# Taylor-softmax attention and a quantised FFN: rows and sums moved through HBM buffers, z formed on ScalarE

## What is computed

```python
h  = layernorm(x) ; h = layernorm(h) * ln_w + ln_b
q, k, v = heads(h @ w_q), heads(h @ w_kv[:, :256]), heads(h @ w_kv[:, 256:])   # 16 heads of 16
q, k = rope(q, theta), rope(k, theta)
s = q @ k.T / 4
t = 1 + s + 0.5 * s * s                    # Taylor instead of exp
x = x + layernorm(((t / t.sum(-1)) @ v) @ w_o)
g = layernorm(x)                           # FFN: both sides to a 6-bit grid in blocks of 32
x = x + layernorm(quant(g) @ quant(weight).T + bias)
```

## Time and profile before

| | |
|---|---|
| time, median of 3 runs | 648.65 us (647.7 to 649.6) |
| the profiled execution's own time | 651.11 us |
| its span, first to last instruction | 648.8 us |
| mean granted TensorE clock | 0.985 of full |
| TensorE, VectorE, ScalarE, GpSimd busy | 615.9, 594.8, 530.0, 449.3 us |
| instructions | 20724 |
| moved by DMA | 43.51 MB in 52362 packets |

### The profile page before, as it was taken

The page is one execution under the profiler, slowest core; times in us unless marked ns, Lnnn a source line. Parts: engine busy times, 40 slices in busy tenths (PEclk is TensorE's granted clock), DMA queues, the critical chain, the costliest instruction groups (busy, mean ns, idle before and its releaser), DMA issues. The chain is left out here.

```text
span 648.8 us, 20724 instructions
## 1 busy us (share of the span) xinstructions
PE 615.9 (95%) x6620; PEld 457.7 (71%) x6620; DVE 594.8 (92%) x1489; ACT 530.0 (82%) x1448; POOL 449.3 (69%) x785
## 2 busy tenths in 40 slices
PE   6889999999999999999999999999999999999974
PEld 5666667676776776777777777767777766788763
DVE  5799899899899989999999999989999999987796
ACT  4347788888788897989888888978888888999973
POOL 3475466677777878788777867767877777765464
PEclk9699999999999999999999999999999999999996
DMA  7101031222223232232323232223223212230201
GB/s 245 34 2 42 20 76 30 72 63 65 50 72 88 70 91 68 75 84 67 62 67 83 77 86 73 69 57 101 60 68 92 76 39 41 68 91 18 68 26 49
DMA packets 52362, 43.51 MB, mean 67 GB/s; under 512 B 7201, under 2 KB 48545, under 8 KB 52257
## 3 DMA queue, kind: packets, MB, share of 16 engines
q1 hardware_dynamic: 51440, 41.42, 24.1%
q10 hardware_dynamic: 816, 0.79, 0.4%
HBM read 18.65 MB, written 8.39 MB: 42 GB/s over the span
## 5 line engine op out<-in xcount | busy, mean ns | idle before, releaser
L1168 ACT ACTIVATE feat<-ps_f 128x512 f32<-128x512 f32 x256 | 144.4, 599 | 4.9 <-PE ps_f L852 4.3
L691 DVE TENSOR_TENSOR kf<-kf 128x896 f32<-128x896 f32 (+1 forms) x128 | 131.2, 1027 | 1.8
L852 PE MATMUL ps_f<-qT,selr 128*128 128x512 f32 x320 | 122.1, 435 | 1.8 <-ACT qT L1236 1.3
L691 POOL TENSOR_TENSOR kf<-kf 128x224 f32<-128x224 f32 x64 | 76.5, 1195 | 13.3 <-DVE kf L1515 11.1
L1015 PEld LDWEIGHTS ps_mt<-kf,vp 128*32 128x32 f32 x2048 | 64.1, 110 | 30.0 <-issue 28.3
L1015 PE MATMUL ps_mt<-kf,vp 128*32 128x153 f32 x2048 | 79.7, 296 | 0.6 <-DVE kf L691 0.6
L1725 POOL TENSOR_TENSOR qsp<-kf,qsp 128x256 fp32r<-128x256 f32 x64 | 58.6, 916 | 9.8 <-ACT qsp L1259 9.6
L852 PEld LDWEIGHTS ps_f<-qT,selr 128*128 128x128 f32 x320 | 52.8, 190 | 15.2 <-issue 11.0
L913 PE MATMUL ps_o<-feat,main 120*32 120x512 f32 x448 | 59.7, 604 | 0.0
L916 PE MATMUL ps_o<-feat,rm 128*32 128x512 f32 x448 | 58.6, 593 | 0.0
L788 PE MATMUL ps_qk<-wkqv_h,hT_l 128*128 128x512 f32 x128 | 52.4, 409 | 3.3 <-DVE wkqv_l L1425 3.3
(11 more groups left out here) (199 smaller groups left out, 1885.2 us busy)
## 6 DMA issues: line engine op xcount, KB each, us to landing
xc<-L_attn_x SPq DMA_DIRECT2D x16, 512.0 KB, 4.5
result<-fin SPq DMA_DIRECT2D x64, 128.0 KB, 2.0
xa<-L_attn_x SPq DMA_DIRECT2D x15, 512.0 KB, 4.1
heads_out<-osb SPq DMA_DIRECT2D x224, 32.0 KB, 2.0
shares<-sums SPq DMA_DIRECT2D x112, 64.0 KB
sums<-osb SPq DMA_DIRECT2D x224, 2.0 KB
wkqv<-L_attn_w_kv ACTq DMA_DIRECT2D x2, 256.0 KB, 4.9
xa<-L_attn_x SPq DMA_DIRECT2D x1, 384.0 KB, 6.2
```

Source lines behind the costliest of these rows:

```text
L691: return eng.tensor_tensor(dims(row, F_MAIN, [[FW, heads], [HD, NR - 1], [1, HD]]), dims(row, F_LIN, [[FW, heads], [0, NR - 1], [1, HD]]), ...
L852: pe.matmul(ps_f[i % 2][:, :], selr[:, i], queries, start=True, stop=True).then_inc(sel_done, 1)
L1168: act.activation(feat[:, p2, i], ps_f[i % 2][:, :], ACT.Square).then_inc(squared, 1)
```

## The change

It has five parts. (1) move_quad stores a whole quad of osb, 256 KB, in one transfer to an HBM buffer rows. After four quads the new fetch_heads reads the sums (one transfer) and the heads (two) from it; the new store_inverses stores the inverted sums to an HBM buffer inverses, and spread_shares reads them from there, each head's row 16 times, in two transfers. That makes 4 + 3 + 1 + 2 = 10 transfers a sequence. copy_quad now waits for the quad's store alone. (2) normalise_x runs on ScalarE as an Identity with a column of scales and one of biases; the bias is minus mean times inverse root, a new GpSimd stage shift_x. (3) constant and rest_terms are cut in two stages each. (4) IDLE has 14 fills of two products in the first steps and one drain near the end. (5) ORDER is new for all engines; the pitch of TensorE's cycle is 58 as before.

```diff
-        "attend": ((43, 54, 65, 76, 90, 101, 114, 127, 140, 154, 168, 183, 198,), (25, 39, 53, 69,), (474, 489, 503,
...
+        "attend": ((43, 55, 67, 78, 87, 104, 114, 126, 139,), (24, 38, 52, 68,), (285, 300, 314, 330, 344, 358, 373,
...
-IDLE = {"fill": (), "drain": ()}
+IDLE = {"fill": (2, 2, 2, 4, 4, 6, 7, 10, 10, 14, 14, 19, 24, 32,), "drain": (943,)}
...
+        rows = nc.dram_tensor("rows", [2, NQ, P, T], F32).ap()
+        inverses = nc.dram_tensor("inverses", [H * T // P, P], F32).ap()
...
+        centre_x = sb("centre_x", [P, 2])
...
+                spread(n, "store_inverses", store_inverses)
+                spread(n, "fetch_heads", fetch_heads)
...
-                par, quad, s = t.par, t.tile, t.seq
-                if quad == 0:
-                    wait(sp, norm_ready, NT * (s - 1))
-                    for tile in range(NT):
-                        wait(sp, shares_in[tile], 16 * CH * s)
+                par, quad = t.par, t.tile
+                wait(sp, heads_in[par], 16 * CH * (t.load - 1))
+                wait(sp, sums_in, 16 * (t.seq - 1))
                 sp.wait_ge(o_copied, t.n)
-                for part in range(NT):
-                    sp.dma_start(sums[part * H + HQ * quad:part * H + HQ * (quad + 1)],
-                                 osb[HD:P:VW, par, quad, part * P:(part + 1) * P]).then_inc(sums_in, 16)
-                for h in range(HQ):
-                    row = HD * (HQ * (quad % 2) + h)
-                    sp.dma_start(heads_out[row:row + HD, par, quad // 2], osb[VW * h:VW * h + HD, par, quad]).then_inc(heads_in[par], 16)
+                sp.dma_start(rows[par, quad], osb[:, par, quad]).then_inc(moved[par], 16)
+            def fetch_heads(t):
+                par, s = t.par, t.seq
+                wait(sp, inverses_out, 16 * s)
+                sp.wait_ge(moved[par], 16 * NQ * t.load)
+                by_row = rows[par].rearrange("q (h r) n -> (q h) r n", r=VW)
+                sp.dma_start(sums[:, :], by_row[:, HD]).then_inc(sums_in, 16)
+                wait(sp, norm_ready, NT * (s - 1))
+                for c in range(CH):
+                    sp.dma_start(heads_out[:, par, c], by_row[c * HC:(c + 1) * HC, 0:HD]).then_inc(heads_in[par], 16)
+            def store_inverses(t):
+                s = t.seq
+                for c in range(CH):
+                    wait(sp, shares_in[c], 16 * s)
+                sp.wait_ge(inverted, s + 1)
+                sp.dma_start(inverses, sums[:, :]).then_inc(inverses_out, 16)
...
                 s = t.seq
+                sp.wait_ge(inverses_out, 16 * (s + 1))
                 wait(sp, norm_ready, NT * s)
-                sp.wait_ge(inverted, s + 1)
-                for tile in range(NT):
-                    for c in range(CH):
-                        first = tile * H + c * HC
-                        sp.dma_start(shares[:, c, tile * P:(tile + 1) * P],
-                                     dims(sums[first:first + HC, 0:1], 0, [[0, HD], [1, P]])).then_inc(shares_in[tile], 16)
+                for c in range(CH):
+                    sp.dma_start(shares[:, c], dims(inverses, c * HC * T, [[0, HD], [1, T]], [T, HC])).then_inc(shares_in[c], 16)
...
+            def normalise_x(t):
+                act.wait_ge(x_centred, t.n)
+                wait(act, zT_done, t.n - 2)
+                act.activation(z[:, t.two, 0:D - 1], xa[:, t.par, t.tile, 0:D - 1], ACT.Identity,
+                               bias=centre_x[:, t.two:t.two + 1], scale=rs["x"][:, t.two:t.two + 1]).then_inc(z_ready, 1)
...
-                wait(act, sums_in, 16 * NQ * NT * (t.seq - 1))
-                wait(act, heads_in[par], 16 * H * (t.load - 1))
+                wait(act, moved[par], 16 * NQ * (t.load - 1))
...
+                each(n, "normalise_x", normalise_x)
...
                 wait(dve, z_ready, t.n - 2)
+                wait(dve, x_centred, t.n - 2)
                 dve.bn_aggr(mv[:, t.two], st[:, t.two]).then_inc(means, 1)
...
-            def normalise_x(t):
-                dve.wait_ge(rstd["x"], t.n)
-                wait(dve, zT_done, t.n - 2)
-                dve.tensor_scalar(z[:, t.two, 0:D - 1], xa[:, t.par, t.tile, 0:D - 1], mv[:, t.two, 0:1], rs["x"][:, t.two:t.two + 1],
-                                  ALU.subtract, ALU.mult).then_inc(z_ready, 1)
...
+            def sum_linear(t):
+                dve.wait_ge(mt_copied, t.seq + 1)
+                wait(dve, cb_ready, t.seq)
+                dve.tensor_reduce(lins[:], mts[:, :, F_LIN:NF], AX.X, ALU.add).then_inc(lins_done, 1)
             def constant(t):
-                dve.wait_ge(mt_copied, t.seq + 1)
-                dve.tensor_reduce(lins[:], mts[:, :, F_LIN:NF], AX.X, ALU.add).then_inc(lins_done, 1)
                 dve.wait_ge(lins_done, t.seq + 1)
...
-            def rest_terms(t):
+            def scale_terms(t):
...
                 dve.tensor_scalar(rest[:, :, HD:VW], mts[:, :, F_LIN:NF], ALPHA / 2, None, ALU.mult).then_inc(lins_scaled, 1)
+            def rest_terms(t):
                 dve.wait_ge(lins_scaled, t.seq + 1)
...
             def invert_sums(t):
-                dve.wait_ge(sums_in, 16 * NQ * NT * (t.seq + 1))
+                dve.wait_ge(sums_in, 16 * (t.seq + 1))
                 dve.reciprocal(sums[:], sums[:]).then_inc(inverted, 1)
...
-                    dve.wait_ge(heads_in[t.par], 16 * H * t.load)
-                    dve.wait_ge(shares_in[t.tile], 16 * CH * (t.seq + 1))
+                    dve.wait_ge(heads_in[t.par], 16 * CH * t.load)
+                    for c in range(CH):
+                        dve.wait_ge(shares_in[c], 16 * (t.seq + 1))
...
             def rstd_x(t):
+                wait(pool, z_ready, t.n - 2)
                 inverse_root("x", t)
+            def shift_x(t):
+                pool.wait_ge(rstd["x"], t.n)
+                wait(pool, z_ready, t.n - 2)
+                pool.tensor_scalar(centre_x[:, t.two:t.two + 1], mv[:, t.two, 0:1], rs["x"][:, t.two:t.two + 1], -1.0,
+                                   ALU.mult, ALU.mult).then_inc(x_centred, 1)
```

More of the change, by code:

```diff
@@ new lines @@
+    "sequence", "scale_ln": "once", "scale_terms": "sequence", "sines": "once", "split_ffn_weight": "once", "split_wo":
+    "once", "spread_shares": "spread", "store_inverses": "spread", "sum_bias": "once", "sum_linear": "sequence",
+    "sum_wo": "once", "tables": "once", "turn_attention": "tail", "turn_ffn_weight": "once", "turn_quads": "tail",
+    "turn_sums": "sequence", "turn_weights": "once", "warm_up": "once", "weight_cast_high": "once", "weight_cast_low":
+    "once", "weight_choice": "once", "weight_distance_sizes": "once", "weight_distances": "once", "weight_high": "once",
```

504 lines of the change are left out of this document (257 added, 247 removed), and 96 rows, old and new, of the table ORDER.

## The result

The changed kernel took **658.1 us** (median of 4 runs, 655.0 to 659.5) where the kernel before took 648.2 beside it: a ratio of 1.015, 95% interval 1.0098 to 1.0202. It is slower by 1.5%; the forecast was 633 us, its range 618 to 652. The profiled execution took 656.7 us with a span of 655.1, and all rows of after are from it.

What follows compares the result with a forecast made beforehand. VectorE was taken to set the pace, TensorE right behind. The profiled 651.1 us - 15 (z's move) - 0 (moves) - 1 (idle products) = 635.1, less 2.5 for the runs' median: 633 us, range 618 to 652.

Steps and rivals of the forecast that it cites:

- TensorE needs 8.59 + 0.30 = 8.89 and loses 0.20 us a tile: TensorE's time for a tile without waiting, from spacings of starts, against 9.09 us a tile; the rest lost to other engines.
- VectorE sets the pace: The steady middle: VectorE, with 3% idle time, limits the kernel, and TensorE stands right behind it.
- TensorE is the wall: Rival: TensorE's 99.3% busy middle is real, leaving only clock and share-wait gains; 646 to 650 us, chance 0.10.
- Normalising the stream leaves VectorE: 64 instructions, 29.7 us busy, leave VectorE; gain between 11 and 29.7 us, taken as 15 us.
- the emptiest of the three: ScalarE, taking over z, rises to at most 93% busy from 250 to 550 us; price on the path nothing.
- ScalarE answers too late: Rival: squares, high parts and copies wait behind z on ScalarE, taking 8 of 16 us away; 641 us, chance 0.17.
- others would get shorter with z gone: Operations that z stretches, by a port pair shared between VectorE and GpSimd, would shorten, tending to 618 us.
- (b): From the reciprocal's start to the shares landing through HBM: 5.5 to 7.6 us against 6.6 in the order; cost 0.
- way through HBM is late: Rival: two shares land one after the other, VectorE waits 5.1 us a sequence; 695 us, 666 at 3 us; chance 0.16.
- (a): From the last copied quad to the reciprocal, through HBM: 5.2 to 7.3 us, covered by 9 to 17 us.
- SyncE behind its new waits: Results to store stand behind waits of fetch_heads and store_inverses on SyncE: nothing, or 7 us if the lead is short.
- Idle products: 28 added TensorE products in the first tiles keep the clock up: 1 us of gain, 4 either way.

Runs made afterwards that it cites:

- the shares off the chain: Changed kernel, with each sequence's shares fetched from the reciprocals of the sequence before (wrong values): 646.9 us, 0.9993 against the kernel before.
- in halves: Changed kernel, with shares read from HBM in four transfers of 128 KB instead of two of 256 KB, att waiting for its own half: 647.2 us, 1.0011.
- VectorE at 79% and no share late: Changed kernel with shares of the sequence before and VectorE's two products of keys a tile cut to one head each from the third tile: 639.4 us, 0.9908.
- the best version: Changed kernel with shares spread from SBUF in eight transfers and two places of SyncE's order swapped: 643.2 us, 0.9948 against the kernel before.
- the swaps: Changed kernel with all forty old moves, two result tiles issued ahead of the eight issues of shares on SyncE: 655.3 us, against 670.1 without.
- two close neighbours: Changed kernel with shares from SBUF in eight transfers (657.8 us), and with all forty old moves (670.1 us), both before SyncE's order was altered.

## Why the prediction was wrong

The forecast was 25 us too low. With the shares off the chain, or in halves, the kernel takes 647: so 11 us are the way of the shares. The other 14 are a gain that didn't come out, since 647 is only level with before. No run parts these 14 between z's move and the new order, but the runs show where the forecast's reasoning broke.

**"TensorE needs 8.59 + 0.30 = 8.89 and loses 0.20 us a tile": this step failed.** It took 8.89, put together from the shortest spacings of one tile, for a pace that TensorE can reach once VectorE serves it sooner. With VectorE at 79% and no share late, TensorE did 219 selection products in 400 us, 400 / 43.8 = 9.13 us a tile, at 99% busy; before, 217 took 9.22. Only with less work on TensorE and VectorE both, 225, was it 8.89. Whether the 9.13 are TensorE's own work or also hand-overs isn't shown (VectorE waits 42.3 us for ScalarE's high part there, and a busy share of 99% doesn't tell); either way the 8.89 weren't to be had by relieving VectorE. So some 0.09 to 0.12 us a tile were to be had from VectorE's side, 5 to 7 us in 55 tiles, and not the 11 to 29.7 between which the forecast put its 15. The 0.20 itself is a difference of two measures: 9.09 is a count of whole tiles between fixed times, where the starts give 9.25, and the forecast's own rows with their waits give 8.93 + 0.30 = 9.23. The first half, "VectorE sets the pace", fits: the kernel before gained 9 us from an eighth less on TensorE. The rival "TensorE is the wall", given 0.10, has the number that the changed kernel reaches without its late shares (646 to 650), but not quite the mechanism: less work on TensorE alone doesn't move it much either.

**"Normalising the stream leaves VectorE ... 15 us": mis-sized, because of that step.** The steady rate of the best version is that of before (217 and 217, or 9.20 and 9.25). In the new order z's place on ScalarE is worth 14 us, but this only pays back a part of what the order takes; in the old order it costs 27. The forecast priced ScalarE's place in its queue by its busy share (93%, "the emptiest of the three") and at 0 on the path. In the old order the cost lay in what stands behind z while ScalarE waits for GpSimd's shift (28.3 us), which a busy share doesn't show. There the rival "ScalarE answers too late" was the right mechanism, and its 8 us were too small; in the changed kernel the same wait is 7.1 us, and VectorE's waits for ScalarE came with the order. z's own duration, 604 ns, was right but for a few ns (0.51 to 0.60). That others would get shorter with z gone didn't show on VectorE: its busy time fell by 24.8 us, z's own was 29.7.

**The order had no term.** I priced the parts as if they were edits to the order that was there. The parts in the old order cost 27 and 79 us, the order without them 35, all together 10. No sum of parts gives this. Part of the 35 is SyncE's stalls before results, of which the swaps removed 15 us in the kernel with the old moves; what else the order takes, and on which engine, is open.

**"(b) ... 5.5 to 7.6 us ... I take 0": mis-sized.** Measured 9.5 us in the stretch shown, 8.4 to 11.6 in the 14 sequences: the last term, 2.0 to 4.1 us for the shares, was 5.9 there and 5.2 to 6.0 in three stretches. The store, taken at 2.0, was 1.8 at the least and 4.7 at the most. The room was larger than forecast: the 6.6 us leave out the reciprocal's own 0.93, which (b) counts, so they should have been 7.5, and in the trace VectorE had 7.0 to 9.1 us of work there, 7.8 in the mean. By the forecast's own account, waits for shares against the 9.1 of before, 14.0 - 9.1 makes 5 us more, inside its -9 to +12. The whole of the way, taken off, gave 11. This is the rival "way through HBM is late", at 14.0 / 14 = 1.0 us a sequence instead of the 1.8 from which it would decide against the relief; with the relief missing, it decided. Its reason, two shares landing one after the other, is supported, if not proven: in halves the loss is gone.

**"(a) ... covered": right here**: the changed kernel's VectorE waited 0.6 us for sums, once. It holds by the new order only; in the old one VectorE waited 13 us for sums.

**"SyncE behind its new waits: nothing": right for this kernel**, and luck. In two close neighbours results behind a wait of SyncE cost 15 us.

**"Idle products ... 1 us": right in kind**, 2.6 measured.

## What to carry to other kernels

When two or three engines are nearly full, moving work from the fullest is worth the distance to the next, which is measured by shortening that next one too, and not by the work moved. A transfer that feeds the first of several tiles should be cut so that the first tile waits for its own part alone, and a store of results should be issued ahead of anything in its queue that waits. In a kernel with an order written out, compare a part only inside an order made for it.

## What the runs showed of the hardware

Two transfers of 256 KB, each of 2 KB rows in HBM read 16 times over, were 5.93 us on their way from the first one's issue, while one load of 512 KB, each row read once, landed after 4.6 us in the same execution:

```profile
xa<-L_attn_x SPq DMA_DIRECT2D x15, 512.0 KB, 4.6
sums<-rows SPq DMA_DIRECT2D x14, 32.0 KB, 2.7
```

Whether the repeated reads, the second issue or other traffic is the reason wasn't tried. The Trainium skill ("DMA: Bandwidth & Descriptors", Anatomy of one DMA) puts some 2 us into every transfer whatever its size, for transfers that GpSimd issues. Those here are SyncE's; the stores of 32 KB to HBM agree with a least of 1.8 us and a median of 2.1, but not with their 4.7 where another transfer had just been issued, and the read of 32 KB back at 2.7 is above it.

A TensorE that the windows show 98 to 99% busy gave only 7 to 9 us for an eighth less work. With 28 products of 128 columns added at the start and nothing else changed, the granted clock from 18 to 28 us was 1.00 instead of 0.50, worth 2.6 us. And two stands of TensorE behind a wait of 4.5 and 4.9 us on VectorE were each followed by a stretch at a lower granted clock, 0.66 over 5 us and 0.57 over 8.
